# Edge projection beside the first scatter pass, padded lookup tiles and an accumulator kept by products

## The chip, the cores and the metric

The kernel runs on one NeuronCore of one Trainium2 chip. The metric is the device time of one execution in microseconds; lower is better. The core has five engines with an in-order instruction stream each: TensorE (PE; its weight loads are listed as PEld), VectorE (DVE), ScalarE (ACT), GpSimd (POOL) and SyncE (SP, which here only issues DMAs). They meet through semaphores.

## What is computed

A graph network of four layers on one graph of 3125 nodes (256 values each) and 103125 edges, with 18 or 64 attributes, a type and a weight per edge. Each layer normalizes x, gathers rows by edge, and sums messages by node:

```python
N, E = 3125, 103125
edge_index = jnp.stack([src, dst])
h = jnp.maximum(_layernorm(x, axis=-1), 0.0)
x = x + _L0_gnn_ref(h, edge_index, edge_attr_18, ...)       # softmax over the edges of src
h = jnp.maximum(_layernorm(x, axis=-1), 0.0)
x = x + _L1_gnn_ref(h, edge_attr_64, edge_weight, ...)      # softmax over the edges of dst
h = jnp.maximum(_layernorm(x, axis=-1), 0.0)
x = x + _L2_gnn_ref(h, ..., src, dst, edge_type_8)          # typed sum, batch norm
h = jnp.maximum(_layernorm(x, axis=-1), 0.0)
x = x + _L3_gnn_ref(h, src, dst, ...)                       # attention over dst

# inside _L1_gnn_ref, what the change touches:
    ep = ef @ We + be                                       # (E, 64) @ (64, 32)
    scores = jnp.einsum('ehd,ehd->eh', q[dst], k[src] + ep[:, None, :]) * scale
    scores = scores * ew[:, None]
    m = jax.ops.segment_max(scores, dst, num_segments=n)
    ex = jnp.exp(scores - m[dst])
    s = jax.ops.segment_sum(ex, dst, num_segments=n)
    out = jax.ops.segment_sum((ex / s[dst])[:, :, None] * v[src], dst, num_segments=n)
```

## The kernel before

**Sorting.** `sort_all` brings the edges into the order of src and then of dst, by counting. A node number is split into a block (25 of them, `NB`) and a place in it (126, in tiles of P = 128). Edges lie in tiles of 128, and a step is G = 8 tiles; 101 steps (`ISTEPS`) cover all edges. The function runs these blocks one after the other; each ends when all engines have ended their part:

1. Loading (to L321). SyncE loads src, dst, type and weight, each by one main load (L288), five loads of a column each (`RCOL`, L291) and a short last one (L292); then x (L296, L297) and the weights of the edge projection and of the first node projection (L300 to L302). Behind the first two VectorE makes the keys (L316 to L321).
2. Histogram (L374 to L495). Per step VectorE writes two sets of one-hot rows, block (`hi`, 25 wide, L338) and place (`lo`, 128 wide, L340), into a buffer of two rounds of four steps; TensorE counts a round by 32 products of them into one bank (L423, waits for `hist_ready`, signals `hist_used`). Beside it runs the edge projection, edge_attr_64 times We: SyncE loads `feat` (L407), TensorE turns a step by four transposes (`turn`, L434), multiplies by `duo_w` in four products (`multiply`, L443), ScalarE copies the turned tiles (`take`) and the products (`stage`), and stores them to `projected` in DRAM, which layer 1 reads. At the end VectorE and TensorE make the start of each node's segment (`lay_out`, L346 on; `lay_out_sums`, L465).
3. First scatter pass, `scatter(keys_of[0], ..., FirstPass)`: each edge's record is written to its place in the order of src. Step b: SyncE waits until the scatters of step b-2 have landed (L524) and loads the attributes (L526). TensorE turns the block one-hots (L642, copied by ScalarE, L564), spreads the keys (L654, compared by VectorE, L608). Then comes the table chain, four times per step (d = 0 to 3, two tiles each): ScalarE copies the table from PSUM (L577), TensorE updates it with two products (L670) and looks two tiles up in the copy with f32 products over 25 rows (L675), and VectorE picks the base out of each (L616). From rank and base VectorE makes the eight positions (L625), and GpSimd issues eight indirect DMAs, one per tile (L545). `FirstPass` also counts the histogram of the other key: VectorE makes `next_hi` and `next_lo`, TensorE counts them (L717) at d = 3 in bank SPARE. Its hooks `sync`, `tensor_table` and `scalar` are empty. At the start ScalarE issues a DMA that fills the second order's record array with blanks (17120 KB).
4. Second scatter pass, with `SecondPass`, in the order of dst; beside it the layer norm of x and its projection to q, k and v (products of 512 columns) run, spread over the steps.

**Layers.** `edge_layer(kind)` runs layers 0, 1 and 3 (`kind` 0, 1, 3) over 107 steps of eight tiles (T = 856) in sorted order. GpSimd gathers rows of `kv` by indirect DMA (L1120), TensorE expands q by edge (`expand`, L1187 and L1190), VectorE makes key products and weighted messages (L1509, L1476) and scans for maxima (L1444), ScalarE exponentials and one-hots; then TensorE sums messages by node, two tiles per pair into a bank (`sums`, L1230), ScalarE copies the four pair sums to `pair_sums` (`move_sums`, L1357; the last two rows of each go to DRAM, L1360), and VectorE adds each into `acc`, at the pair's block (`add_sums`, L1465). TensorE's order of a step is `expand(2)`, `turn_scores`, `sums(0)` of two steps ago, `expand(3)`, `turn_back`, `expand(0)` of the next step, `sums(1)`, `expand(1)`, `front`. In `expand` the bank goes round; VectorE's key products read it. Layer 2 has its own loop and isn't touched.

## Time and profile before

| | |
|---|---|
| median of 3 runs | 8586.36 us (8586.0 to 8587.62) |
| profiled execution, its own time | 8571.41 us |
| span in its trace | 8569.7 us |
| mean granted TensorE clock | 0.784 |
| TensorE busy | 6613.0 us (77%) |
| VectorE busy | 5308.7 us (62%) |
| ScalarE busy | 3576.5 us (42%) |
| GpSimd busy | 5221.6 us (61%) |

Busy shares are means over stages which have different limits, so they are read by stretch: loading until 55 us, histogram until 285, first scatter pass until 1333, second until 2394, then the layers. The page's line of 40 slices shows the same: the granted TensorE clock stands at 5 tenths through the scatter passes and at 8 to 9 later.

```profile
PE   7999998999979989974777777667855555667675
...
DVE  6677776666657777774999999721122223455556
...
POOL 0477776777767777721777777200277775677772
PEclk9655555555589999997999999879877777887887
```

### The profile page before, as it was taken

Reading aid. Unit: us, or ns where it says so; the run is one execution under the profiler, and the core shown is the slowest. Engines: PE = TensorE matmul, PEld = TensorE weight load, DVE = VectorE, ACT = ScalarE, POOL = GpSimd, SP = SyncE. Lnnn points to the kernel's source line nnn. Section 1 sums busy time; section 2 is a strip of 40 time slices with the busy share of each in tenths; the row PEclk is TensorE's granted clock in tenths of the full one; section 3 lists DMA queues with packets and bytes.
Section 4 is the critical chain, followed back from the end, with each engine's and each line's share of the span. In section 5 each row is a group of like instructions: output and inputs, shape, how many; then the busy total and the mean of one; then the engine's idle time right before and its main releaser. Section 6 shows DMA issues by size and latency. Waiting matters only on the chain. (4 is left out here: it accounts for less than half of the span.)

```text
span 8569.7 us, 143502 instructions
## 1 busy us (share of the span) xinstructions
PE 6613.0 (77%) x33110; PEld 4732.5 (55%) x33111; DVE 5308.7 (62%) x15263; ACT 3576.5 (42%) x10766; POOL 5221.6 (61%) x5120
## 2 busy tenths in 40 slices
PE   7999998999979989974777777667855555667675
PEld 6777775666646666652555555455433344445454
DVE  6677776666657777774999999721122223455556
ACT  3322222333347666632666666223200000777772
POOL 0477776777767777721777777200277775677772
PEclk9655555555589999997999999879877777887887
DMA  7411111111145555532666666200344443444442
GB/s 219 136 17 16 17 17 26 33 33 34 33 106 140 138 136 138 140 61 96 184 175 175 176 178 175 85 11 33 132 108 108 108 108 80 107 110 109 109 108 47
DMA packets 1013468, 849.20 MB, mean 99 GB/s; under 512 B 751678, under 2 KB 841581, under 8 KB 1009339
## 3 DMA queue, kind: packets, MB, share of 16 engines
q0 software_dynamic: 257152, 645.64, 27.7%
q1 hardware_dynamic: 710069, 154.62, 9.1%
q10 hardware_dynamic: 45780, 44.08, 1.5%
q14 instruction: 341, 2.79, 0.1%
q8 instruction: 126, 2.06, 0.1%
HBM read 723.28 MB, written 120.67 MB: 98 GB/s over the span
## 5 line engine op out<-in xcount | busy, mean ns | idle before, releaser
L1120 POOL DMA_INDIRECT edges_kv<-kv,edges_rec x1712 | 1998.4, 1167 | 968.0 <-issue 511.0
L1230 PE MATMUL banks<-edges_kv,edges_hot 128*128 128x288 f32 (+2 forms) x5136 | 1563.8, 455 | 623.3 <-DVE edges_kv L1476 412.9
L1230 PEld LDWEIGHTS banks<-edges_kv,edges_hot 128*128 128x128 f32 x5136 | 1051.9, 215 | 1005.0 <-issue 563.6
L1631 POOL DMA_INDIRECT edges_rows<-rel,edges_rec x856 | 809.3, 945 | 965.2 <-DMA edges_rec<-by_dst_records 710.0
L545 POOL DMA_INDIRECT by_src_records<-sort_by_src_rec,sort_pos_i x808 | 773.9, 958 | 544.2 <-issue 533.2
L1120 POOL DMA_INDIRECT edges_kv<-feat,edges_rec x856 | 829.3, 969 | 270.4 <-issue 253.9
L675 PE MATMUL banks<-sort_table,sort_hot_hi_t 25*128 25x128 f32 x3232 | 952.1, 444 | 52.0 <-DVE sort_junk L616 47.2
L1647 PE MATMUL banks<-edges_rows,edges_hot 128*128 128x256 f32 x1712 | 625.8, 529 | 466.1 <-DMA edges_rows<-rel,edges_rec 449.2
L545 POOL DMA_INDIRECT by_dst_records<-sort_by_dst_rec,sort_pos_i x808 | 773.7, 958 | 288.0 <-issue 250.3
L1465 DVE TENSOR_TENSOR acc<-edges_pair_sums,acc 128x288 f32 (+2 forms) x1284 | 560.6, 437 | 487.0 <-DMA edges_kv<-feat,edges_rec 268.7
L675 PEld LDWEIGHTS banks<-sort_table,sort_hot_hi_t 25*128 25x128 f32 x3232 | 721.5, 307 | 221.2 <-issue 121.1
L1647 PEld LDWEIGHTS banks<-edges_rows,edges_hot 128*128 128x128 f32 x1712 | 428.0, 262 | 664.3 <-issue 404.0
L616 DVE SCALAR_TENSOR_TENSOR sort_junk<-banks,sort_hot_lo 128x128 bf16<-128x128 f32 x1616 | 435.3, 287 | 578.0 <-PE banks L675 537.5
L1330 ACT ACTIVATE edges_off<-columns,edges_column 128x128 bf16<-128x128 f32 x2568 | 784.6, 390 | 0.0
L1679 DVE TENSOR_TENSOR agg<-banks,agg 128x256 f32 x428 | 181.7, 424 | 768.8 <-PE banks L1647 768.8
L1302 ACT ACTIVATE edges_apart<-banks,minus_p 128x512 bf16<-128x512 f32 x642 | 429.3, 686 | 435.0 <-PE banks L1142 226.8
L608 DVE SCALAR_TENSOR_TENSOR sort_junk<-banks,sort_key_cur,sort_earlier 128x128 bf16<-128x128 f32 x1616 | 575.6, 411 | 6.0 <-PE banks L654 6.0
L1357 ACT COPY edges_pair_sums<-banks 128x288 f32<-128x288 f32 (+2 forms) x1284 | 460.7, 383 | 275.6 <-PE banks L1230 246.8
L1476 DVE TENSOR_TENSOR edges_kv<-edges_kv 128x1024 f32<-128x1024 f32 x428 | 518.8, 1212 | 0.0
L577 ACT COPY sort_table<-banks 25x128 f32<-25x128 f32 x808 | 204.8, 254 | 728.2 <-PE banks L670 728.2
L564 ACT COPY sort_hot_hi_t<-banks 25x512 f32<-25x512 f32 x404 | 231.9, 574 | 647.2 <-PE banks L642 647.2
L1190 PE MATMUL banks<-x,edges_hot_t 128*128 x1712 | 476.5, 403 | 3.4 <-DVE edges_kv L1509 3.4
(372 smaller groups left out, 12506.6 us busy)
## 6 DMA issues: line engine op xcount, KB each, us to landing
edges_kv<-kv,edges_rec POOLq DMA_INDIRECT x1712
sort_feat<-in_edge_attr_dram SPq DMA_DIRECT2D x100, 256.0 KB, 3.6
rel<-tables_stage SPq DMA_DIRECT2D x25, 1008.0 KB
by_dst_records<-by_dst_blank ACTq DMA_DIRECT2D x1, 17120.0 KB, 54.2
edges_rec<-by_dst_records SPq DMA_DIRECT2D x107, 160.0 KB
edges_rows<-rel,edges_rec POOLq DMA_INDIRECT x856
edges_kv<-feat,edges_rec POOLq DMA_INDIRECT x856
by_src_records<-sort_by_src_rec,sort_pos_i POOLq DMA_INDIRECT x808, 2.1
```

The source lines that it names most:

```text
L545: pool.indirect_dma_start(O.rec, bass.IndirectOffsetOnAxis(ap=pos_i[:, u, c:c + 1], axis=0), rec[:, u, c, :], None).then_inc(scattered[u], 16)
L608: last = dve.scalar_tensor_tensor(out=junk[:, 0, c, 0:P + mates].rearrange("p (t e) -> p t e", e=P), in0=ps[:, 4 + h, end - P - mates:end] ...
L675: pe.matmul(ps[:, 2 + c % 2, 0:P], hot_hi_t[:, u, c, :], table[:, d % 2, :], start=True, stop=True).then_inc(looked_up, 1)
L1120: pool.indirect_dma_start(kv[:, r, c, 0:koff + DIM], None, tab, bass.IndirectOffsetOnAxis(ap=reci[:, r, c, idx:idx + 1], axis=0)).then_inc ...
L1190: last = pe.matmul(out[:, c, 2 * P - QW:2 * P], hot_t[:, b % 2, 2 * m + c, :], rows, start=(kind == 1), stop=(kind == 1 or c == 1), skip_g ...
L1230: last = pe.matmul(ps[:, 6 + m % 2, 0:OW], hot[:, b % 2, c, :], kv[:, b % BUFS, c, koff:koff + OW], start=(c % 2 == 0), stop=(c % 2 == 1))
L1330: last = act.activation(off[:, c, :], C.columns[:, c % 2, :], ACT.Abs, bias=column[:, b % 2, c:c + 1], scale=-1.0)
L1357: act.copy(pair_sums[:, m, :], ps[:, 6 + m % 2, 0:OW]).then_inc(sums_copied, 1)
L1465: dve.tensor_tensor(rows, pair_sums[:, m, :], rows, ALU.add).then_inc(added, 1)
L1476: dve.tensor_tensor(v4, v4, bc(exps, dh), ALU.mult).then_inc(msg_done, 1)
L1631: pool.indirect_dma_start(rows[:, b, c, :], None, tab, bass.IndirectOffsetOnAxis(ap=reci[:, b, c, idx:idx + 1], axis=0)).then_inc(gathered ...
L1647: last = pe.matmul(ps[:, m, 0:DIM], hot[:, b, c, :], rows[:, b, c, :], start=(c % 2 == 0), stop=(c % 2 == 1))
```

## The change

1. Loading: the five column loads of each array become one (`PARTS = 3`). The loads of x and of the weights move from the loading block to the block of the histogram. GpSimd clears three more tiles.
2. Histogram: the projection leaves it. VectorE writes into `hot_hi` and `hot_lo`, two steps deep, and TensorE counts each step for itself.
3. First scatter pass: `FirstPass` gets the projection. SyncE loads `feat` behind the attribute load of the same step (two buffers). TensorE turns half a step at d = 0 and half at d = 2, and multiplies the half before; ScalarE copies both at d = 1 and d = 3 and issues the store at d = 1. The count of the other histogram moves to the table bank's columns 128 to 255, two tiles at each d, before the table's own products.
4. Both passes: `hot_hi`, `hot_hi_t` and `table` get 128 columns or rows in place of 25, the rest zero; lookups (L675) run over 128 rows, turns (L642) and table products (L670) give 128 rows.
5. Layer 1 (`kind == 1`): a product of the identity with `acc`'s block is added in PSUM to each pair's sum (`with_past`), after a wait for the copy of the pair before (`acc_kept`). ScalarE copies the sum back to `acc` and rows 96 to 127 of it to `pair_sums`. VectorE's additions are gone.

```diff
-        hot_hi = ph.sbuf("hot_hi", [P, 2, G, NB], BF16)
+        hot_hi = ph.sbuf("hot_hi", [P, 2, G, P], BF16)
-        hot_hi_t = ph.sbuf("hot_hi_t", [NB, 2, G, P])
+        hot_hi_t = ph.sbuf("hot_hi_t", [P, 2, G, P])
-        table = ph.sbuf("table", [NB, 2, P])
+        table = ph.sbuf("table", [P, 2, P])
...
-        feat = ph.sbuf("feat", [P, ROUND, G, FA])
-        feat_t = ph.sbuf("feat_t", [P, 2, HALF, P])
+        feat = ph.sbuf("feat", [P, 2, G, FA])
+        feat_t = ph.sbuf("feat_t", [P, 2, P])
...
-        PARTS = RCOL + 2
+        PARTS = 3
...
+                pool.memset(table[:], 0.0).then_inc(filled, 1)
+                pool.memset(hot_hi_t[:], 0.0).then_inc(filled, 1)
+                pool.memset(hot_hi[:], 0.0).then_inc(filled, 1)
...
-                    for g in range(RCOL):
-                        sp.dma_start(tile[:, MAIN + g:MAIN + g + 1], rest[g]).then_inc(loaded[k], 16)
+                        sp.dma_start(tile[:, MAIN:MAIN + RCOL], dram[MAIN * P:MAIN * P + RCOL * P].rearrange("(g p) -> p g", p=P)
+                                     ).then_inc(loaded[k], 16)
...
+                def body(j, b):
+                    dve.wait_ge(hist_used[b], j)
+                    position_ones(dve, keys_of[0], hot_hi[:, b, :, 0:NB], hot_lo[:, b], bass.ds(j * (2 * G) + b * G, G), hist_ready)
...
+                def body(j, b):
+                    pe.wait_ge(hist_ready, j * 4 + 2 * b + 2)
+                    for c in range(G):
+                        last = pe.matmul(ps[0:NB, 0, 0:P], hot_hi[:, b, c, 0:NB], hot_lo[:, b, c, :],
+                                         start=False, stop=False, skip_group_check=True)
+                    last.then_inc(hist_used[b], 1)
...
-                            last = pe.matmul(ps[0:NB, 0, P * c:P * c + P], hot_hi[:, b % 2, 4 * h + c, :], C.ident_b[:],
+                            last = pe.matmul(ps[:, 0, P * c:P * c + P], hot_hi[:, b % 2, 4 * h + c, :], C.ident_b[:],
...
-                                last = pe.matmul(ps[0:NB, TABLE, 0:P], hot_hi[:, u, c, :], hot_lo[:, u, c, :],
+                                last = pe.matmul(ps[:, TABLE, 0:P], hot_hi[:, u, c, :], hot_lo[:, u, c, :],
...
         class FirstPass:
             def sync(sp, j, b, tail):
-                pass
+                u = b % 2
+                if not opening(j, b, 2):
+                    sp.wait_ge(feat_made, at(j, b)(2, 0) - 2)
+                if not tail:
+                    sp.dma_start(feat[:, u], rows_main(feat_dram)[:, bass.ds(at(j, b)(G, 0), G), :]).then_inc(feat_in[u], 16)
...
+            def tensor_table(cls, pe, j, b, d, tail):
+                if opening(j, b, 1):
+                    return
+                if d == 0:
+                    pe.wait_ge(next_ready, at(j, b)(2, 0))
+                last = cls.count(pe, (b + 1) % 2, (2 * d, 2 * d + 1))
+                if d == PAIRS - 1:
+                    last.then_inc(next_used, 1)
...
+            def turn(pe, j, b, h, tail):
+                u = b % 2
+                if h == 0:
+                    pe.wait_ge(feat_in[u], turn_of(j, b) * 16 + 16)
+                for i in range(2):
+                    c = 4 * h + 2 * i
+                    last = pe.transpose(ps[:, SPARE, P * i:P * i + P], feat[:, u, c:c + 2, :].rearrange("p c a -> p (c a)"), C.ident[:])
...
             def tensor(cls, pe, j, b, d, tail):
+                if d == 0:
+                    if not opening(j, b, 1):
+                        pe.wait_ge(feat_taken, n(2, 0))
+                        cls.multiply(pe)
+                    cls.turn(pe, j, b, 0, tail).then_inc(feat_made, 1)
+                if d == 2:
+                    pe.wait_ge(feat_taken, n(2, 1))
+                    cls.multiply(pe)
+                    cls.turn(pe, j, b, 1, tail).then_inc(feat_made, 1)
...
+            def scalar(cls, act, j, b, d, tail):
+                n, u = at(j, b), b % 2
+                if d == 1:
+                    act.wait_ge(feat_made, n(2, 1))
+                    if not opening(j, b, 1):
+                        cls.take_products(act, 1 - u, 1)
+                    cls.take_turned(act).then_inc(feat_taken, 1)
+                    if not opening(j, b, 1):
+                        act.wait_ge(feat_taken, n(2, 1))
+                        act.dma_start(rows_main(projected)[:, bass.ds(n(G, 0) - G, G), :], feat_out[:, 1 - u]).then_inc(feat_stored[1 - u], 16)
+                if d == 3:
+                    act.wait_ge(feat_made, n(2, 2))
+                    act.wait_ge(feat_stored[u], turn_of(j, b) * 16)
+                    cls.take_products(act, u, 0)
+                    cls.take_turned(act).then_inc(feat_taken, 1)
...
+                def with_past(j, b, m):
+                    if not (first_steps(j, b, 1) and m == 0):
+                        pe.wait_ge(acc_kept, n(PAIRS, m))
+                    pe.matmul(ps[:, 6 + m % 2, 0:OW], C.ident[0:BN, :],
+                              acc[0:BN, bass.ds(block, 1), :].rearrange("p o w -> p (o w)"), start=False, stop=True).then_inc(summed, 1)
...
                     if oldest:
                         sums(*oldest, 0)
+                        if kind == 1:
+                            with_past(*oldest, 0)
                     if inside:
                         expand(j, b, (3,))
+                    if oldest and kind == 1:
+                        with_past(*oldest, 1)
...
                     if oldest:
                         sums(*oldest, 1)
+                        if kind == 1:
+                            with_past(*oldest, 2)
                     if ahead:
                         expand(*ahead, (1,))
                     if beyond:
                         front(*beyond)
+                    if oldest and kind == 1:
+                        with_past(*oldest, 3)
...
+                        if kind == 1:
+                            act.copy(acc[:, bass.ds(blocks[m], 1), :].rearrange("p o w -> p (o w)"), ps[:, 6 + m % 2, 0:OW]
+                                     ).then_inc(acc_kept, 1)
+                            act.copy(pair_sums[ENDS:P, m, :], ps[ENDS:P, 6 + m % 2, 0:OW]).then_inc(sums_copied, 1)
+                            continue
```

## Rows read from the trace of the kernel before

**Rows 1.** Stretches, both scatter passes: us; busy PE, PEld, DVE, ACT, POOL; clock; DMA; GB/s.
```profile
285.00:1332.60 1047.60, 973.10 (x5583) 730.00 (x5581) 769.80 (x3699) 272.47 (x1193) 773.88 (x808) 0.50 0.16 28
...
1359.60:2394.30 1034.70, 939.46 (x4918) 647.07 (x4918) 668.78 (x3662) 312.58 (x1465) 773.68 (x808) 0.54 0.16 33
```

**Rows 2.** Timeline, loading stage: start, duration, engine, line, [idle before <-releaser].
```profile
11.26 6.81 SPq L291 DMA_DIRECT2D sort_src_i<-in_src_dram  x5
...
24.56 0.58 DVE L316 TENSOR_SCALAR sort_lo_i<-sort_src_i 128x808 int32<-128x808 int32 x1 [6.89 <-DMA sort_src_i<-in_src_dram]
...
32.99 12.84 SPq L297 DMA_DIRECT2D x<-in_x_dram  x1
...
33.67 0.58 DVE L321 TENSOR_SCALAR sort_by_dst_seg<-sort_dst_i 128x808 f32<-128x808 int32 x1
...
54.92 1.76 SPq L407 DMA_DIRECT2D sort_feat<-in_edge_attr_dram  x4
```

**Rows 3.** Timeline, histogram stage: two pair starts, one count, the end.
```profile
73.22 3.59 PE L423 MATMUL banks<-sort_round_lo,sort_round_hi 128*25 128x128 bf16 x32
...
79.79 0.35 DVE L338 TENSOR_TENSOR sort_round_hi<-banks,sort_by_src_hi 128x200 bf16<-128x200 f32 x1
...
81.19 0.35 DVE L338 TENSOR_TENSOR sort_round_hi<-banks,sort_by_src_hi 128x200 bf16<-128x200 f32 x1
...
263.04 0.28 DVE L346 COPY sort_hist<-banks 25x128 f32<-25x128 f32 x1 [7.77 <-PE banks L465]
```

**Rows 4.** Waits over 55 to 263 us: who waits for whom, us, count, longest.
```profile
DVE sort_round_hi L338 <- PE banks L423: 55.0, 24, 9.4
```

**Rows 5.** Timeline, one step of the first scatter pass.
```profile
1186.62 0.96 POOL L545 DMA_INDIRECT by_src_records<-sort_by_src_rec,sort_pos_i  x1 [0.31 <-issue]
...
1188.48 0.39 PE L670 MATMUL banks<-sort_hot_lo,sort_hot_hi 128*25 128x128 bf16 x2
...
1188.99 10.40 SPq L526 DMA_DIRECT2D sort_by_src_rec<-in_edge_attr_dram  x2
...
1189.01 1.22 PE L675 MATMUL banks<-sort_table,sort_hot_hi_t 25*128 25x128 f32 x4
...
1196.10 0.17 DVE L625 TENSOR_TENSOR sort_pos_i<-sort_base,sort_rank 128x8 int32<-128x8 f32 x1 [0.21 <-DVE sort_junk L616]
```

**Rows 6.** DMA issues: count, KB each, median us from issue to landing.
```profile
sort_feat<-in_edge_attr_dram SPq DMA_DIRECT2D x100, 256.0 KB, 3.6
```

**Rows 7.** Timeline, from positions to first gather in the first pass.
```profile
1009.70 0.17 DVE L625 TENSOR_TENSOR sort_pos_i<-sort_base,sort_rank 128x8 int32<-128x8 f32 x1 [0.21 <-DVE sort_junk L616]
...
1010.67 0.96 POOL L545 DMA_INDIRECT by_src_records<-sort_by_src_rec,sort_pos_i  x1 [0.43 <-issue]
```

**Rows 8.** Timeline: transposes early in the histogram, lookups after a projection product.
```profile
65.72 1.06 PE L434 MATMUL banks<-ident,sort_feat 128*128 128x128 f32 x4
...
1418.45 0.71 PE L675 MATMUL banks<-sort_table,sort_hot_hi_t 25*128 25x128 f32 x4
```

**Rows 9.** Stretches: after a projection product; inside the histogram.
```profile
1418.30:1421.70 3.40, 2.65 (x23) 1.87 (x22) 2.53 (x18) 1.67 (x11) 2.79 (x3) 0.98 0.07 18
...
100.00:262.00 162.00, 161.77 (x1704) 149.63 (x1702) 115.60 (x162) 78.15 (x169) 0.00 (x0) 1.00 0.67 199
```

**Rows 10.** Stretch: the edge stage of layer 1, steady part.
```profile
4200.00:5400.00 1200.00, 911.42 (x4194) 674.85 (x4193) 1117.36 (x1859) 753.40 (x2047) 926.11 (x745) 0.94 0.64 176
```

**Rows 11.** Groups, layer 1, 4200 to 5400 us: busy, mean ns | idle before.
```profile
L1230 PE MATMUL banks<-edges_kv,edges_hot 128*128 128x272 f32 x1488 | 432.0, 438 | 288.6 <-issue 152.0 <-DVE edges_kv L1476 136.2
...
L1465 DVE TENSOR_TENSOR acc<-edges_pair_sums,acc 128x272 f32 x372 | 159.3, 428 | 0.0
...
L1357 ACT COPY edges_pair_sums<-banks 128x272 f32<-128x272 f32 x372 | 132.0, 380 | 57.4 <-PE banks L1230 50.3
```

**Rows 12.** Timeline, layer 1: an addition and what follows it.
```profile
4708.13 0.43 DVE L1465 TENSOR_TENSOR acc<-edges_pair_sums,acc 128x272 f32 x1
...
4708.48 0.41 DVE L1444 TENSOR_TENSOR_SCAN edges_run_max<-edges_pen,banks 64x128 f32<-64x128 f32 x1
```

235 lines of the change are left out of this document (90 added, 145 removed).

## The prediction

> **What bounds the kernel now.** I read the table of stretches first, for the two scatter passes. In the second one GpSimd issues 808 indirect DMAs in 1034.7 us, 1.28 us each, and every other engine has air: that pass is GpSimd's own pace. The first pass has the same 808 and takes 1047.6 us, 10.37 us for each of its 101 steps against 10.24 [rows 1]. TensorE is busy there for 973 of 1047.6 us at a granted clock of 0.50, so two things of nearly equal length run side by side: the gathers' 10.24 and a chain through TensorE, ScalarE and VectorE of 10.3 to 10.4. Then the loading stage, in order of time: VectorE has keys from 24.56 on, but SyncE is held by the load of x (12.84 us) and the next stage begins only at 54.9 [rows 2]. In the histogram the VectorE pairs follow each other at 1.40 us per step; still the stage ends at 263.04, because TensorE also does the edge projection there and VectorE waits 55.0 us in 24 waits for its counts [rows 3, 4]. Last the edge stage of layer 1: in its steady 1200 us there are 93 steps (372 additions at L1465, 4 a step), 12.9 us each; VectorE is busy 1117 us, 93%, TensorE 911 us, ScalarE 753 us, GpSimd 926 us plus its gaps [rows 10, 11]. VectorE is the bound, with GpSimd close.
>
> **The loading stage.** Five column loads per key array become one, and x and the weights go to the next block. SyncE spent 6.81 us on issuing the five columns of src, and VectorE started at 24.56, when the last src load had landed [rows 2]; one column load in place of five should spare about 6 us of that, and VectorE start near 18.5. Its two key conversions took 24.56 to 34.25 with a wait between (the last, L321, starts at 33.67 [rows 2]), so they end near 27.5 and the histogram starts 27 us earlier (22 to 30: the one column load has as many elements as five had, so its own issue may be longer). x is now issued while VectorE builds one-hots; nothing waits for it before the second pass. The three new GpSimd clears lie beside the loads. -27.
>
> **The histogram.** Without projection, VectorE sets the pace: 101 x 1.40 = 141.4 us, plus 3 at the ends, instead of the 208 us from 54.96 to 263.04 [rows 3]. Now that only two steps are buffered, a count of 8 products must end before VectorE has done the next step: 32 took 3.59 us at their slowest [rows 3], so 0.9 and two hand-overs, below 1.40, with little to spare. -63 (-50 if every step loses 0.13). Both together: -90.
>
> **The first pass, where the projection now is.** Per step it adds to TensorE four transposes (the same four took 1.06 us before the clock rose [rows 8]) and four products of about the same length, and to ScalarE two copies of each kind and a store. What counts more is a new wait. SyncE's loop first waits for the scatters of step b-2 to land, issues the attribute load of b, and only then the load of feat for b. TensorE needs that feat right after the first lookups of step b, in the same in-order queue as the table chain. So: scatter b-2, feat load, rest of step b's chain, scatter b. Round the loop: from the first to the last gather of b-2 7 x 1.28 = 9.0 us; from the last gather (1186.62) to SyncE's next issue (1188.99) 2.4; the feat issue behind the attribute load 0.4 (an estimate); landing 3.2 (less than the median of 3.6 in the histogram, where the DMAs had more to do [rows 6]); the rest of the chain R; and 0.8 from the positions (ready at 1009.87) to the first gather at 1010.67 [rows 5, 7]. R before is from 1188.48 to 1196.27, 7.8 us at the lower clock, none of it idle TensorE to speak of; with transposes and products 9.8. At the upper clock a set of lookups takes 0.71 instead of 1.22 us [rows 5, 8], so all of R times 0.58 is 5.7. The loop covers two steps: (15.8 + R) / 2 = 12.8 us per step at the lower clock, 10.75 at the upper, against 10.37 now.
>
> **Which clock.** The tall and wide shapes don't shorten an operation by themselves. The row that matters is the clock: 0.50 in the first pass with TensorE busy 93% on products of 25 rows or 25 columns [rows 1]; 1.00 in the histogram with transposes and products of 128x128 f32 between the narrow counts; and 0.98 in the short stretch after a full 512-column product of the second pass [rows 9]. So busy time alone does not raise it here, full-size work does, and after the change nearly all lookups and turns are full-size. But the new loop leaves TensorE idle for 3 to 4 us in each step, until feat lands, and the work after such a gap starts at the lower level. I take half of R's saving lost after the gap, less what comes back late in it: R = 7.2, hence 11.5 us per step. 101 x (11.5 - 10.37) = +114 us (bounds +38, all at the upper clock, and +245, all at the lower). Start: the blank fill of by_dst saturates the DMAs beside the first steps, so their feat loads land late: +12 (0 to 20). The last stores lie beside the last gathers: 0.
>
> The Trainium skill (TensorE: Matmul & The Clock Gate, "Why this matters for your kernels") asks only for continuous TensorE work to reach the full clock, and warns that an idle gap between bursts brings the lower one back. The first half would have the first pass warm already, and the tall shapes worth nothing; the granted 0.50 there says otherwise, and the measurement decides. The second half is the third rival below, at its 12.8 us.
>
> **The second pass** gets the same shapes and nothing else. It is at GpSimd's pace and stays there: 0 (+-3).
>
> **Layer 1's accumulator by product.** VectorE loses four additions per step; what follows one begins 0.35 us after it [rows 12], so 1.4 of 12.0 busy us, leaving 10.6. TensorE gains four products with the identity, 8 instructions; the same kind at L1230 takes 432.0/1488 = 0.29 us each [rows 11], so 2.3 on top of 911/93 = 9.8: 12.1. ScalarE gains four copies of 0.38 at most [rows 11] on top of 8.1: 9.6. The additions no longer queue behind VectorE's work, but product m now waits for ScalarE's copy of product m-1, and behind that wait stand, on TensorE, the next expansions, which VectorE's key products need. In the present order an expansion (about 1 us) lies between each two, which covers a copy of 0.38 us. So TensorE takes VectorE's place: I take 12.2 us, 107 x (12.2 - 12.9) = -75. Bounds: -150 if all 1.4 us come through; +30 if the copies' wait is exposed (0.3 us a step). GpSimd's gathers there take 926/745 = 1.24 us.
>
> The Trainium skill (SBUF — State Buffer, "SBUF: two separate sides") says a VectorE operation with two SBUF inputs, which these additions are, can lock GpSimd out for its length. The trace agrees so far that a gather takes 1.24 us beside them against 0.96 in the passes; by the rule the gathers would get shorter and the gain nearer the upper bound.
>
> **Sum.** -90 + 114 + 12 - 75 = -39 on the profiled execution's 8571.4 us (span 8569.7 and 1.7 around it): 8532. The median of the runs shown is 15 us above that execution, so 8547; I say **8545 us**.
>
> **Rivals.** (A) The forecast, 0.43. (B) The feat load is hidden: the clock stays up, the loads land in 2.5 us, the loop falls under GpSimd's 10.24, and the first pass ends like the second: -90 - 13 + 12 - 75 = -166, 8420 us. For it: 10.75 is near 10.24, and a faster TensorE makes its own slack. Against: 9.0 + 2.4 + 0.8 of the loop are fixed. 0.20. (C) Slower than before: the gap keeps TensorE at the lower clock through the step, 12.8 us per step: -90 + 245 + 12 - 75 = +92, 8678 us. For it: the 0.50 of both passes now. Against: without a gap left to wait in, there would be more full-size work per microsecond than now. It decides from 10.37 + (90 + 75 - 12)/101 = 11.9 us per step. 0.20. (D) The accumulator gives nothing, since TensorE with its chain of ScalarE copies is as late as VectorE was: 12.9 us again, +36, 8622 us. For it: 12.1 us of TensorE work leaves 0.8 for all its waits, and it had 3.1 idle. Against: its present idle time waits for VectorE, which gets faster. 0.12. What is left, 0.05, is a histogram that runs off its 1.40.
>
> **Chances.** A run of this kernel can tell 0.2% (17 us) from no change. A lies around -39 with some 35 either way: of its 0.43 about 0.32 is faster, 0.09 the same, 0.02 slower. B is faster, C slower, D half same, half slower. Together: faster 0.56, same 0.16, slower 0.28. The range leaves out the outer half of B's and C's errors: 8420 to 8690.
>
> **What would show it.** Histogram: VectorE's pairs at 1.40 us and the first scatter near 195 us. First pass: steps of 11.5 us in the position additions; TensorE idle for 3 to 4 us before the first transposes, ended by the DMA of feat; gathers idle before each eighth; a granted clock of 0.7 to 0.9, in place of 0.50. Second pass: 1035 us, clock well above 0.54. Layer 1: steps of 12.2 us, VectorE under 90% busy and waiting for products of L1190, TensorE over 90%. The prediction falls if SyncE's feat load is not what the first transposes wait for, if the clock sticks at one level, or if layer 1's steps stay at 12.9.

## The result, and the profile after

| | before | after |
|---|---|---|
| median of 4 runs | 8586.18 us (8579.67 to 8587.62) | 8639.69 us (8627.75 to 8646.84) |
| profiled execution | 8571.41 us | 8646.5 us |
| span, mean granted clock | 8569.7 us, 0.784 | 8644.7 us, 0.847 |

The ratio is 1.0063, with a 95% interval of 1.0048 to 1.0079: the change makes the kernel slower by 0.6%, 54 us in the medians and 75 us between the two profiled executions. The forecast was 8545 us, 41 us faster. The stretches below come from the profiled executions, so they hold 21 us more than the medians do.

The two traces are compared by landmarks: the first and last indirect DMA of each pass, and the first instruction of the block behind layer 1.

| stretch | before, us | after, us | difference | forecast |
|---|---|---|---|---|
| start to first scatter | 285.0 | 195.4 | -89.6 | -90 |
| first scatter pass | 1047.6 | 1229.0 | +181.4 | +126 |
| second pass, with what lies before it | 1061.7 | 1056.3 | -5.4 | 0 |
| to the first gather of layer 1 | 1647.4 | 1639.6 | -7.8 | 0 |
| layer 1, first gather to the next block | 1398.7 | 1387.8 | -10.9 | -75 |
| rest, which the change doesn't touch | | | +7.3 | 0 |

The stretches of the kernel after that answer to [rows 1, 10]: busy us of PE, PEld, DVE, ACT and POOL, then granted clock, DMA share, GB/s.

```profile
195.40:1424.40 1229.00, 865.79 (x6789) 705.89 (x6789) 780.46 (x3699) 360.54 (x1596) 776.19 (x808) 0.75 0.25 57
1449.00:2480.80 1031.80, 675.24 (x4918) 562.66 (x4918) 652.12 (x3658) 312.73 (x1464) 775.97 (x808) 0.76 0.16 33
4200.00:5400.00 1200.00, 1074.46 (x5007) 790.93 (x5005) 1039.02 (x1515) 914.72 (x2455) 801.95 (x756) 0.98 0.65 180
```

TensorE has more instructions in the first pass than before (6789 against 5583), and is busy for less time, 866 us against 973: the clock is 0.75 in place of 0.50. Yet the pass is 181 us longer. In the second pass, where only the shapes changed, TensorE's time falls from 939 to 675 us and the pass stays at GpSimd's pace.

The first two stages went as forecast. The timeline of the kernel after: the column load of src, the first key conversion, the start of the next block, two of VectorE's pairs, the end of the histogram.

```profile
11.28 1.26 SPq L289 DMA_DIRECT2D sort_src_i<-in_src_dram  x1
...
20.19 0.58 DVE L306 TENSOR_SCALAR sort_lo_i<-sort_src_i 128x808 int32<-128x808 int32 x1 [1.98 <-DMA sort_src_i<-in_src_dram]
...
28.38 0.37 DVE L371 CAST sort_duo_f<-sort_duo_i 25x428 f32<-25x428 int32 x1 [0.31 <-PEq L263]
...
33.69 0.36 DVE L320 TENSOR_TENSOR sort_hot_hi<-banks,sort_by_src_hi 128x200 bf16<-128x200 f32 x1
35.09 0.36 DVE L320 TENSOR_TENSOR sort_hot_hi<-banks,sort_by_src_hi 128x200 bf16<-128x200 f32 x1
...
175.42 0.28 DVE L328 COPY sort_hist<-banks 25x128 f32<-25x128 f32 x1 [1.23 <-PE banks L404]
```

Against [rows 2, 3]: the column load is issued in 1.26 us in place of 6.81, VectorE starts at 20.2 (forecast 18.5), the block at 28.4 in place of 54.9. The pairs follow each other at 1.40 us and nothing stops them; the histogram ends at 175.4 in place of 263.0.

In the first pass, this is one step that waits and half of the next. The first row is SyncE's attribute load, the second the feat load behind it.

```profile
872.76 0.17 DVE L536 TENSOR_TENSOR sort_pos_i<-sort_base,sort_rank 128x8 int32<-128x8 f32 x1
...
874.61 0.27 PE L642 MATMUL banks<-sort_next_lo,sort_next_hi 128*25 128x128 bf16 x2 [1.83 <-DVE sort_next_lo L322]
...
875.93 0.38 SPq L437 DMA_DIRECT2D sort_by_src_rec<-in_edge_attr_dram  x1
...
876.59 0.34 SPq L615 DMA_DIRECT2D sort_feat<-in_edge_attr_dram  x1
...
879.42 0.69 PE L665 MATMUL banks<-ident,sort_feat 128*128 128x128 f32 x2 [3.11 <-DMA sort_feat<-in_edge_attr_dram]
...
887.58 0.17 DVE L536 TENSOR_TENSOR sort_pos_i<-sort_base,sort_rank 128x8 int32<-128x8 f32 x1 [0.21 <-DVE sort_junk L527]
...
888.59 0.96 POOL L456 DMA_INDIRECT by_src_records<-sort_by_src_rec,sort_pos_i  x1 [3.87 <-DVE sort_pos_i L536]
```

TensorE stands for 3.11 us until feat lands, as forecast for every step; from there to the positions it takes 8.3 us, and GpSimd has been idle for 3.87 us when they come. There is a second wait, 1.83 us, that the prediction didn't name: the count of the other histogram now stands at the head of the step (d = 0), and needs the one-hots that VectorE writes behind its positions of the step before. TensorE's waits from 600 to 1200 us:

```profile
PE banks L642 <- DVE sort_next_lo L322: 95.4, 51, 2.0
PE banks L665 <- DMA sort_feat<-in_edge_attr_dram: 65.8, 25, 5.3
```

The feat wait comes 25 times in these 600 us, so in every second step and not in each, 2.6 us in the mean. A step with it takes 14.8 us, one without it at the upper clock 9.0; they often alternate, and the pair costs 23.8.

The granted clock has two levels here, 1.00 (2.4 GHz) and 0.50 (1.2 GHz). Around the wait of the step shown (columns as above, the clock is the third number from the end):

```profile
872.80:875.50 2.70, 0.89 (x10) 0.81 (x10) 2.67 (x10) 0.41 (x5) 2.09 (x3) 1.00 0.05 9
875.60:879.40 3.80, 0.71 (x4) 0.52 (x3) 2.04 (x8) 0.19 (x2) 2.89 (x4) 0.50 0.49 98
879.42:885.70 6.28, 6.28 (x39) 5.23 (x40) 2.51 (x16) 2.08 (x6) 4.08 (x5) 0.50 0.12 31
```

The clock is already at the lower level when the wait for feat begins (876.3): it fell at 875.5, behind the 1.83 us in which TensorE waited for the one-hots. It stays low over the feat wait and 6.3 us of work behind it.

At the start of the pass there is a hole. The blank fill, and ScalarE's first store of projected rows:

```profile
182.07 0.42 ACTq L180 DMA_DIRECT2D by_dst_records<-by_dst_blank  x1
...
201.19 28.23 ACTq L718 DMA_DIRECT2D edge_projected<-sort_feat_out  x1
...
229.52 0.26 ACT L488 COPY sort_table<-banks 25x128 f32<-25x128 f32 x1 [28.36 <-issue]
...
233.11 0.96 POOL L456 DMA_INDIRECT by_src_records<-sort_by_src_rec,sort_pos_i  x1 [27.71 <-DVE sort_pos_i L536]
```

In layer 1, groups of instructions from 4200 to 5400 us, and below them two score reductions that follow each other in an undisturbed step.

```profile
L1228 PE MATMUL banks<-acc,ident 126*128 x756 | 254.1, 417 | 60.0 <-ACT acc L1364 53.5 <-issue 3.1
...
L1364 ACT COPY acc<-banks 128x272 f32 x378 | 144.1, 381 | 154.6 <-PE banks L1228 137.4 <-DMA ends<-edges_pair_sums 14.9
L1366 ACT COPY edges_pair_sums<-banks 32x272 f32<-32x272 f32 x378 | 143.0, 378 | 9.1
```

```profile
4743.56 2.28 DVE L1547 TENSOR_REDUCE edges_score_raw<-edges_kv 128x64 f32<-128x2048 f32 x1
...
4755.53 2.28 DVE L1547 TENSOR_REDUCE edges_score_raw<-edges_kv 128x64 f32<-128x2048 f32 x1
```

Both kernels have an undisturbed step of about 11.97 us, which is also the median of the 106 steps in both. Only the mean moved, from 12.86 to 12.66. One such step of the kernel before, and two of the kernel after:

```profile
4708.08:4720.05 11.97, 9.20 (x45) 6.86 (x45) 11.97 (x21) 8.16 (x22) 9.25 (x8) 1.00 0.72 191
```

```profile
4743.34:4755.31 11.97, 11.54 (x55) 8.62 (x56) 10.92 (x17) 9.77 (x27) 4.30 (x4) 1.00 0.30 73
4755.31:4767.30 11.99, 11.11 (x53) 7.96 (x51) 10.82 (x17) 9.34 (x26) 9.08 (x7) 1.00 0.61 166
```

Before, VectorE is busy for all of the step. After, no engine is: TensorE comes nearest, with 11.1 to 11.5 us. Per step the products cost 254.1/94.5 = 2.7 us of TensorE (forecast 2.3). And at the end of the layer 10.6 us are lost, from the last scores to the next block 26.4 us in place of 15.8: with nothing left to expand between them, product and copy stand in a row.

```profile
5487.95 0.62 PE L1228 MATMUL banks<-acc,ident 126*128 x2
5488.87 0.39 ACT L1364 COPY acc<-banks 128x272 f32 x1 [1.23 <-PE banks L1228]
...
5489.59 0.72 PE L1228 MATMUL banks<-acc,ident 126*128 x2 [1.01 <-ACT acc L1364]
```

### The profile page after: what moved, and what is told of

It reads as the page before. It is cut to its first block and busy times, and to the rows that moved or that the text cites. A ratio compares the mean times of both kernels' runs of the same rounds, so it can differ in the third digit from the quotient of the medians.

```text
span 8644.7 us, 146268 instructions
## 1 busy us (share of the span) xinstructions
PE 6302.0 (73%) x33965; PEld 4633.2 (54%) x33966; DVE 5189.5 (60%) x14835; ACT 3743.8 (43%) x11397; POOL 5084.2 (59%) x5123
## 5 line engine op out<-in xcount | busy, mean ns | idle before, releaser
L1107 POOL DMA_INDIRECT edges_kv<-kv,edges_rec x1712 | 1850.9, 1081 | 1083.9 <-issue 538.2
L1217 PE MATMUL banks<-edges_kv,edges_hot 128*128 128x288 f32 (+2 forms) x5136 | 1509.2, 443 | 324.7 <-DVE edges_kv L1491 284.3
L587 PE MATMUL banks<-sort_table,sort_hot_hi_t 128*128 128x128 f32 x3232 | 711.9, 356 | 54.1 <-DVE sort_junk L527 54.1
L1480 DVE TENSOR_TENSOR acc<-edges_pair_sums,acc 128x288 f32 (+1 forms) x856 | 378.1, 442 | 480.1 <-DMA edges_kv<-feat,edges_rec 251.4
L587 PEld LDWEIGHTS banks<-sort_table,sort_hot_hi_t 128*128 128x128 f32 x3232 | 576.5, 251 | 73.1 <-DVE sort_junk L527 69.6
L1524 DVE TENSOR_TENSOR edges_kv<-banks,edges_kv 128x256 f32<-128x256 f32 (+1 forms) x856 | 440.0, 552 | 50.9 <-PE banks L1177 20.0
```

Source lines behind the costliest of these rows:

```text
L587: pe.matmul(ps[:, 2 + c % 2, 0:P], hot_hi_t[:, u, c, :], table[:, d % 2, :], start=True, stop=True).then_inc(looked_up, 1)
L1107: pool.indirect_dma_start(kv[:, r, c, 0:koff + DIM], None, tab, bass.IndirectOffsetOnAxis(ap=reci[:, r, c, idx:idx + 1], axis=0)).then_inc ...
L1217: last = pe.matmul(ps[:, 6 + m % 2, 0:OW], hot[:, b % 2, c, :], kv[:, b % BUFS, c, koff:koff + OW], start=(c % 2 == 0), stop=(kind != 1 an ...
L1524: dve.tensor_tensor(k2, by, k2, ALU.mult).then_inc(edges_used, 1)
```

## The experiments

Four open points: what holds the steps of the first pass, what holds its start, whether the padded shapes are worth their place, and what layer 1's products give. Theory 1 is the prediction's loop (scatter of b-2, feat load of b, the chain, scatter of b); its rival is the new wait for VectorE's one-hots.

**Feat load ahead (`early_feat`).** SyncE issues feat of step b before it waits for the scatters of b-2; the load's own condition, `feat_made`, is met long before.

```diff
                         u = b % 2
+                        if beside is FirstPass:
+                            beside.sync(sp, j, b, tail)
                         sp.wait_ge(scattered[u], turn_of(j, b) * P)
...
-                        beside.sync(sp, j, b, tail)
+                        if beside is not FirstPass:
+                            beside.sync(sp, j, b, tail)
```

> The changed kernel, but SyncE issues the feat load of step b before it waits for the scatters of step b-2, not behind the attribute load. Theory 1 (the loop scatter, feat load, chain, scatter sets the first pass): the wait for feat goes, a step costs what those without it cost now, 9.0 us of TensorE's chain at the upper clock, so GpSimd's 10.24 holds; first pass 28 + 101 x 10.24 = 1062 us in place of 1229, time 8473. Rival (the new wait of the count at the head of each step for VectorE's next ones holds it: 1.8 us of idle TensorE in each step, after which the lower clock comes back): steps of 11.2 us, as those steps now that have no feat wait at the lower clock, pass 1160, time 8570.

Measured: 8469.47 us (8467.99 to 8473.42), 0.9877 of before (0.986 to 0.9893). First pass:

```profile
195.30:1253.80 1058.50, 792.86 (x6789) 645.45 (x6789) 774.02 (x3699) 361.18 (x1596) 773.96 (x808) 0.83 0.29 66
```

```profile
PE banks L645 <- DVE sort_next_lo L322: 119.8, 59, 3.5
...
PE banks L668 <- DMA sort_feat<-in_edge_attr_dram: 5.8, 17, 0.5
```

The forecast time of theory 1 was 8473. The pass falls from 1229.0 to 1058.5 us; the wait for the one-hots is still there, and even grows (119.8 us in 600), and costs nothing any more: it is TensorE's slack behind GpSimd. The loop through the feat load is shown, and with it that its place in SyncE's queue, not the work, made the change slower. The clock still falls in the steps, behind the wait for the one-hots (848.8 is the end of one of 1.94 us), but comes back sooner:

```profile
847.00:850.40 3.40, 1.52 (x13) 1.30 (x14) 3.37 (x16) 0.88 (x7) 2.66 (x3) 1.00 0.54 110
850.40:853.80 3.40, 3.40 (x20) 2.42 (x21) 3.02 (x15) 1.09 (x4) 2.48 (x4) 0.50 0.05 10
```

**The count later (`late_count`), and both (`early_late`).**

```diff
-                if opening(j, b, 1):
+                if opening(j, b, 1) or d == 0:
                     return
-                if d == 0:
+                if d == 1:
                     pe.wait_ge(next_ready, at(j, b)(2, 0))
-                last = cls.count(pe, (b + 1) % 2, (2 * d, 2 * d + 1))
+                last = cls.count(pe, (b + 1) % 2, ((0, 1, 2), (3, 4, 5), (6, 7))[d - 1])
```

> The changed kernel, but the count of the other histogram is made at d = 1, 2, 3 (3, 3 and 2 tiles) in place of all four, so TensorE waits for VectorE's next ones one lookup later. Theory 1 (the feat loop alone): TensorE waits for feat as much longer as it waits less for the ones; steps stay at 11.9 us, time 8640 within 10. Rival (the ones' wait): 1.8 us less in each step, 10.3, time 8480. Both together: in between, 8560.

> Both edits: feat load ahead of the wait for the scatters, and the count from d = 1 on. Theory 1 and the rival alike: no wait is left on TensorE's side but GpSimd's pace; first pass 28 + 101 x 10.24 = 1062 us, time 8473, and no faster than the early feat load alone if theory 1 is right. A third (it is TensorE's work itself, at the lower clock, that is too long): steps stay over 11 us.

Measured: `late_count` 8633.49 us, 1.0064 (1.0048 to 1.0081), first pass 1222.9 us; `early_late` 8517.75 us, 0.993 (0.9913 to 0.9947), first pass 1103.2 us. TensorE's waits from 600 to 1200 us, of `late_count` and then of `early_late`:

```profile
PE banks L665 <- DMA sort_feat<-in_edge_attr_dram: 145.8, 51, 4.8
```

```profile
PE banks L590 <- DVE sort_junk L530: 51.7, 56, 0.9
PE banks L557 <- DVE sort_hot_lo L322: 51.0, 56, 0.9
PE banks L645 <- DVE sort_next_lo L322: 35.8, 56, 0.7
```

Alone, the later count turns one wait into the other (145.8 us for feat in place of 65.8) and gains nothing: the rival falls. With the early load it costs 45 us of the pass and the time is 8518 for an expected 8473, which neither theory had: TensorE waits 2.5 us per step in three places in place of 2.0 in one, and its steps go through a pattern of eight with a mean of 10.7 us. A reading that was not tried: the counts at d = 0 fill time in which TensorE would wait for VectorE anyway, and at d = 1 to 3 they stand in the chain.

**Store by SyncE (`early_late_store`, then `best_2`).** SyncE stores the projected rows of step b-2 at its step b, ahead of feat, and ScalarE's store goes. `best_2` has it with the early load, the count where the change put it, and layer 1's additions as before.

```diff
                 if not opening(j, b, 2):
+                    sp.wait_ge(feat_taken, at(j, b)(2, 0) - 1)
+                    sp.dma_start(rows_main(projected)[:, bass.ds(at(j, b)(G, 0) - 2 * G, G), :], feat_out[:, u]).then_inc(feat_stored[u], 16)
                     sp.wait_ge(feat_made, at(j, b)(2, 0) - 2)
...
-                    if not opening(j, b, 1):
-                        act.wait_ge(feat_taken, n(2, 1))
-                        act.dma_start(rows_main(projected)[:, bass.ds(n(G, 0) - G, G), :], feat_out[:, 1 - u]).then_inc(feat_stored[1 - u], 16)
```

> As the one with both edits, and the projected rows are stored by SyncE in place of ScalarE. In the changed kernel ScalarE's first store has an issue of 28.23 us, while the blank fill that the same engine issued moves 17 MB. Theory: the issue is held by the fill on ScalarE's own queue, and on SyncE's it is not: the hole of 28 us between the first and the second eight gathers falls to under 5, time 25 lower than with both edits, 8448. Rival: the DMAs are full, whoever issues: the store or the feat load waits just as long, no gain.

> The kernel of early_store_adds again (early feat load, store by SyncE, additions by VectorE in layer 1), on a chip of the first kind. First pass: theory (the 28 us hole comes from ScalarE's store behind the blank fill on its own queue) 1038 us; rival (the DMAs are full whoever issues) 1058 as with the early load alone. Layer 1 from its first gather to the next block: rival of the forecast (the products gave 11 us, TensorE at 11.97 us a step where VectorE was at 11.97) 1399 us; the forecast's theory (the products gave 75) 1460. Time by theory and rival: 8469 - 20 + 11 = 8460.

Measured: `early_late_store` 8502.56 us, 0.9912 (0.9896 to 0.9929), first pass 1083.5 us, 19.7 less than without it; the time is 15 us less, where 25 was expected, and misses the expected 8448, as `early_late` under it had missed its own. `best_2` 8467.78 us (8456.71 to 8492.06), 0.9865 (0.9849 to 0.9882). Its first pass, SyncE's first store, and its layer 1 from first to last gather:

```profile
195.20:1235.00 1039.80, 792.54 (x6789) 644.33 (x6789) 772.88 (x3699) 355.90 (x1596) 774.19 (x808) 0.84 0.29 68
```

```profile
200.20 0.34 SPq L617 DMA_DIRECT2D edge_projected<-sort_feat_out  x1
```

```profile
3934.80:5317.10 1382.30, 1044.80 (x4746) 772.05 (x4747) 1270.01 (x2100) 857.19 (x2319) 1068.58 (x856) 0.93 0.64 175
```

1038 us was expected for the first pass and 1039.8 came; the store's issue takes 0.34 us where ScalarE's took 28.23, and the hole is gone. The fill moves the same 17 MB in both, at the same time, so the issue was held on ScalarE's own queue, behind the fill that it had issued there, and not by busy DMAs. Layer 1 to the next block takes 1412.2 us (1399 was expected), against 1382.9 with the products (`early_feat`) and 1387.8 (the kernel after); the kernel before has 1398.7 with the same additions. By the traces the products are worth 11 to 29 us there, not 75. The 29 is the weaker number: the profiled execution of `best_2` took 8492.06 us, 24 more than its median. By the ratios `best_2` is some 10 us faster than `early_feat`, of which the store is 19, which leaves the products some 9 us, with intervals of 14 us either way. So `best_2` and `early_feat` are the same within their intervals, and both beat the kernel before and the kernel after. The early load, SyncE's store and the products together were run only on the chips of the last part.

**Narrow shapes (`early_narrow_4`).** As `early_feat`, with lookups, turns and table products over 25 rows or columns again.

```diff
-                            last = pe.matmul(ps[:, 0, P * c:P * c + P], hot_hi[:, b % 2, 4 * h + c, :], C.ident_b[:],
+                            last = pe.matmul(ps[0:NB, 0, P * c:P * c + P], hot_hi[:, b % 2, 4 * h + c, 0:NB], C.ident_b[:],
...
-                                last = pe.matmul(ps[:, TABLE, 0:P], hot_hi[:, u, c, :], hot_lo[:, u, c, :],
+                                last = pe.matmul(ps[0:NB, TABLE, 0:P], hot_hi[:, u, c, 0:NB], hot_lo[:, u, c, :],
...
-                                pe.matmul(ps[:, 2 + c % 2, 0:P], hot_hi_t[:, u, c, :], table[:, d % 2, :],
+                                pe.matmul(ps[:, 2 + c % 2, 0:P], hot_hi_t[0:NB, u, c, :], table[0:NB, d % 2, :],
```

> The kernel of early_narrow again (early feat load, old shapes of 25 rows or columns in both scatter passes). Theory (the full-size shapes raise the clock and that makes room for the projection): granted clock of the first pass 0.5, steps of 11.7 us or more, first pass 1210 us, time 8620. Rival (the projection's own full-size work keeps the clock up, the padding is worth nothing): first pass 1060, time 8470.

Measured: 8816.29 us (8812.74 to 8827.09), 1.0277 (1.026 to 1.0295): 347 us slower than the same kernel with padded shapes.

```profile
198.90:1594.70 1395.80, 1225.94 (x6789) 949.38 (x6789) 811.58 (x3699) 363.58 (x1596) 773.91 (x808) 0.56 0.21 49
1621.80:2655.40 1033.60, 937.74 (x4918) 647.62 (x4918) 668.61 (x3660) 312.80 (x1465) 773.85 (x808) 0.54 0.16 33
```

The instructions are the same in number (6789), the clock 0.56 in place of 0.83, TensorE's time 1226 us in place of 793. So the padding holds the clock up. The projection's own full-size transposes and products hardly do: 0.56 with them, 0.50 in the kernel before without. Which of the three padded shapes counts was not separated. The second pass takes the same time at either clock (1033.6 us, and 1029.9 in `early_feat`). Steps of the first are 13.7 us, longer than the 11.7 expected: TensorE is busy for 12.1 and waits 1.4 for the one-hots. Without the padding, the projection makes this pass 348 us longer than it was before the change, far more than it spares in the histogram.

**Short product (`short_past_3`).** The kernel after, with the identity product over 16 of 272 columns; the sum over earlier pairs is left out for the others.

```diff
-                    pe.matmul(ps[:, 6 + m % 2, 0:OW], C.ident[0:BN, :],
-                              acc[0:BN, bass.ds(block, 1), :].rearrange("p o w -> p (o w)"), start=False, stop=True).then_inc(summed, 1)
+                    pe.matmul(ps[:, 6 + m % 2, 0:16], C.ident[0:BN, :],
+                              acc[0:BN, bass.ds(block, 1), 0:16].rearrange("p o w -> p (o w)"), start=False, stop=True,
+                              skip_group_check=True).then_inc(summed, 1)
```

> The kernel of short_past again (the changed kernel with the product of the identity over 16 of 272 columns; the other columns' sum over earlier pairs is left out). Theory (TensorE's work, 11.5 of 11.97 us, bounds the undisturbed step of layer 1): median step 10.8 to 11.2 us, VectorE's, and 80 to 120 us less, 8540. Rival (the chain product, ScalarE's copy, product counts): median step within 0.2 us of 11.97, time 8620 or more.

Measured: 8614.82 us, 1.0038 (1.0026 to 1.0049). Layer 1 takes 1371.6 us to the next block, 16 less; the median step is 11.93 us.

```profile
4200.00:5400.00 1200.00, 1010.13 (x5074) 769.99 (x5072) 1052.01 (x1528) 926.95 (x2489) 841.86 (x767) 0.96 0.65 182
```

```profile
L1228 PE MATMUL banks<-acc,ident 126*128 x766 | 131.0, 246 | 51.5 <-ACT acc L1365 46.3 <-issue 3.3
```

The products' time halves, by 1.3 us per step (less than the 2 expected: over 16 columns one still takes 246 ns), and the wait for ScalarE's copy stays (46.3 us against 53.5). TensorE's share falls from 90% to 84%. The time misses the theory's 8540 and comes near the rival's 8620, and so does the median step. But the median hides what happened: 50 of the 106 steps are now under 11.8 us, most of them between 11.2 and 11.6, where the kernel after has 16 (two score reductions that follow each other stand below), and the 106 together are 19 us shorter (mean 12.48 us), of which the end of the layer gives 3 back. So TensorE's work does hold the undisturbed step in part, by some 0.5 us; it is not worth the 80 to 120 us of the theory. That the rest hangs on the chain over ScalarE's copy was argued and not tried; the pauses on top of the undisturbed steps stay open too.

```profile
4662.84 2.28 DVE L1548 TENSOR_REDUCE edges_score_raw<-edges_kv 128x64 f32<-128x2048 f32 x1
...
4674.15 2.28 DVE L1548 TENSOR_REDUCE edges_score_raw<-edges_kv 128x64 f32<-128x2048 f32 x1
```

**On other chips.** Eleven of the eighteen runs fell on three chips on which the kernel before itself takes 10324 to 10430 us. VectorE has pauses of up to 14 us there, and ScalarE of up to 18, whose end the trace puts down to no instruction of the core: about one of VectorE's in each step of the two scatter passes, and none before them. GpSimd's issues are as long as ever (0.96 us), and a step of the second pass takes 13.9 to 14.1 us in place of 10.2. What the pauses are stays open. The ratios to the kernel before on the same chip:

| kernel | ratios, with intervals |
|---|---|
| early load, store by SyncE | 1.0009 (0.9989 to 1.0029), 1.0057 (1.0036 to 1.0078), 1.0041 (1.0026 to 1.0056) |
| the same with additions (`early_store_adds`) | 1.0056 (1.0034 to 1.0079) |
| kernel after with additions (`adds_back`) | 1.0026 (1.0003 to 1.0049), 1.0117 (1.008 to 1.0154) |
| early load, narrow shapes | 1.0046 (1.0022 to 1.007), 1.0123 (1.0097 to 1.015), 1.0127 (1.0103 to 1.0152) |
| short product | 1.0017 (0.9994 to 1.004), 1.0099 (1.0073 to 1.0125) |

The edit of `adds_back`, beside taking out `with_past` and its copies in ScalarE's `move_sums`:

```diff
-                    if kind == 1:
-                        gone = None
```

What was expected, in the order of the three chips:

> The changed kernel with the early feat load, the count left where the change puts it, and the projected rows stored by SyncE. Theory (the early load gives 160 us and SyncE's store another 20, as it did behind the two edits together): first pass 1038 us, time 8449. Rival (SyncE's store, which comes ahead of feat in the queue, delays the loads in every step): first pass longer than with the early load alone, time over 8470.

> The changed kernel with layer 1's accumulator as before: VectorE adds the pair sums, no product with the identity. The forecast's theory (the products spare 75 us): time 8639 + 75 = 8714. Rival (from the two traces: layer 1 from its first gather to the next block takes 1387.8 us against 1398.8, so the products give 11 us): 8650, steps at 12.86 us in place of 12.66.

> The early feat load, but lookups, turns and table products of both scatter passes in their old shapes, 25 rows or columns. Theory (full-size shapes raise the clock, and the clock is what makes room for the projection): the granted clock of the first pass falls from 0.84 to 0.5 to 0.6, TensorE's work per step, 9.6 us before the change, grows by the projection's 2, so steps of 11.7 us or more: first pass 1210 us, time 8620; second pass 0.54 again and still 1030. Rival (the projection's own transposes and products keep the clock up, the padding is worth nothing): first pass 1060, time 8470.

> The changed kernel, the product of the identity with the accumulator made over 16 of its 272 columns, all waits and copies as they are; for the other columns the sum over earlier pairs is left out. Theory (TensorE's own work bounds layer 1's steps now, 2.7 us of it in these products): 2 us less work per step, steps at VectorE's 11.0 to 11.5 us plus the stalls, 100 to 130 us less, time 8525. Rival (the chain product, ScalarE's copy, next product is what counts, not the length of a product): steps within 0.2 us of now, time 8620 or more.

> The kernel of early_store again, on a chip where the kernel before takes 8.58 ms (on the last one it took 10.32, and nothing could be told). Theory (the early load gives 160 us and SyncE's store another 20): first pass 1038 us, time 8449. Rival (the store ahead of feat in SyncE's queue delays the loads in every step): time over 8470.

> The kernel of adds_back again. The forecast's theory (the products spare 75 us): the changed kernel's 8640 + 75 = 8715. Rival (from the two traces: they spare 11 us): 8650, steps of layer 1 at 12.86 us in place of 12.66.

> The kernel of early_narrow again. Theory (the full-size shapes raise the clock and that makes room for the projection): granted clock of the first pass falls from 0.84 to 0.5 to 0.6, steps of 11.7 us or more, first pass 1210 us, time 8620. Rival (the projection's own full-size work keeps the clock up): first pass 1060, time 8470. In the slow chip's traces the clock of the second pass can't decide it, since there the waits were others.

> The kernel of short_past again (the product with the identity over 16 of 272 columns; the other columns' sum over earlier pairs is left out). Theory (TensorE's work bounds layer 1's steps): steps of 11.0 to 11.5 us plus the stalls, 100 to 130 us less, 8525. Rival (the chain of product, ScalarE's copy, product is what counts): steps within 0.2 us, 8620 or more.

> The kernel of early_store a third time, on a chip where the kernel before takes 8.58 ms, it is hoped (on two others it took 10.3 to 10.4). Theory (the early load gives 160 us and SyncE's store another 20): first pass 1038 us, time 8449. Rival (the store ahead of feat in SyncE's queue delays the loads in every step): time over 8470.

> The same with layer 1's accumulator as before, by VectorE's additions. The forecast's theory (the products spare 75 us): 75 us slower than early_store_3, 8524. Rival (they spare 11 us, as the two first traces say): 8460, layer 1 from its first gather to the next block at 1399 us in place of 1388.

> The kernel of early_narrow again, on a chip of the first kind. Theory (the full-size shapes raise the clock and that makes room for the projection): granted clock of the first pass falls from 0.84 to 0.5 to 0.6, steps of 11.7 us or more, first pass 1210 us, time 8620. Rival (the projection's own full-size work keeps the clock up, the padding is worth nothing): first pass 1060, time 8470.

No kernel beats the one before there: every ratio is 1 or above, and the early load with SyncE's store, which was expected at 8449 us, is up to 0.6% slower than the kernel before. The theories can't be judged there: against the kernels with the late feat load on the same chip, the early load with SyncE's store gives 13 to 60 us in place of 190. The order stays, with the narrow shapes last, and so do three things of the traces: the granted clock of the second pass is 0.53 to 0.55 with narrow shapes and 0.66 to 0.67 with padded ones; the end of layer 1 takes 15.8 to 17.5 us with additions and 24.7 to 28.1 with products; the first scatter comes at 195 to 199 us. What the edits are worth depends on the chip.

## Why the prediction was wrong, point by point

**Loading and histogram**: right, -89.6 for -90. The two-step buffer holds: 8 products take 1.03 us and VectorE is never stopped by them.

**The first pass**: the loop was right, and shown by the early load; that every step would wait for feat was not, since the loop covers two steps and its wait comes in one of them. Two sizes failed, one here and one at the start of the pass. The steps' mean without the hole is (1229.0 - 28) / 101 = 11.9 us for a forecast of 11.5, which is +40 us. Of the loop, the two issues and the landing are right (0.66 and 2.8 for 0.4 and 3.2), the last gather to the attribute load is 2.3 for 2.4; the term that failed is R, 8.3 us for 7.2. After the feat wait TensorE is at the lower clock for some 6 us of the 8 (until about 885.7 in the step shown: its pair of transposes takes 0.69 us at 879.42 and 0.39 where the clock is up, the four lookup products 1.17 and 0.66). I had lost half of the saving, which is R = 7.75, and had taken another 0.55 off it with no row behind that. The Trainium skill (TensorE: Matmul & The Clock Gate, "Why this matters for your kernels") warns that a gap between bursts brings the lower clock back. The trace agrees in part: the granted clock is 0.75 in this pass and 0.83 once the feat wait is gone, but in the step shown it had fallen before that gap, behind a wait of 1.83 us, and the gap made the low stretch longer. The wait for VectorE's one-hots, which I had overlooked, turned out to cost nothing in idle time (`late_count`, `early_feat`); the clock falls behind it.

**The start of the pass**: +12 was forecast from feat loads that land late; +28 came, and from another cause. I had costed the projection's stores at nothing, beside the last gathers, and not asked what stands in ScalarE's queue at the first of them: the blank fill. A moved DMA has to be costed in the queue that it is moved into, at its first issue too. This term and R's make up the 55 us between +126 and +181.

**The clock**: right in direction and level, 0.75 in the first pass (0.7 to 0.9 forecast) and 0.76 in the second, and shown by the narrow shapes to be the padding's work. That full-size work raises it needs a limit: the projection's alone left it at 0.56. The padding's worth beside the projection, 347 us, I had put no number on.

**Layer 1**: the step that failed is the subtraction. I set TensorE's 12.1 to 12.2 us of work against 12.9, the mean of the steps before, which holds 0.9 us of pauses; VectorE's undisturbed step was 12.0, and I had that number in the same paragraph. 12.1 against 12.0 is no gain, and the pauses come on top as before. The sum of TensorE's work was itself too high, 11.4 us measured (1074.46/94.5), and the undisturbed step came to 11.97 all the same; `short_past_3` puts some 0.5 us of it down to TensorE, and what else holds it stays open. Rival D (nothing is gained, TensorE with its chain of copies is as late as VectorE was) is nearest to what came, -11 us for its 0, at a chance of 0.12. Left out altogether was the end of the layer, 10.6 us, where the cover named for ScalarE's copy, an expansion, is gone. GpSimd's gathers did get shorter, 801.95/756 = 1.06 us in place of 1.24, and with the additions back 1068.58/856 = 1.25. That agrees with the Trainium skill (SBUF — State Buffer, "SBUF: two separate sides"), that two-input VectorE operations hold GpSimd up; but the gain did not come nearer its upper bound, as the prediction had it by that rule: the median step stayed.

**The sum**: -89.6 + 181.4 - 10.9 and -5.9 in the rest is +75, where -90 + 126 - 75 gave -39. The miss of 114 us is 64 from layer 1 and 55 from the first pass, less 6 from the rest. Either alone would have taken the gain away: with layer 1's term as forecast the sum is +11, with the first pass's +20. "Slower" had stood at 0.28, mostly for a first pass at 12.8 us a step (C); it came at 11.9 and with layer 1's gain missing.

## What to carry to other kernels

A load that is moved into a loop belongs ahead of the waits in its queue that it doesn't need: the same work in the same pass cost 181 us behind one wait and 11 us ahead of it. A change of engine is costed against the bound of the undisturbed step, not against the mean with its pauses, and once more at the ends of the loop, where its cover is missing. Zero padding to full tiles can pay where an engine's clock hangs on it. The clock fell from time to time all the same, also where no wait was longer than 0.9 us (`early_late`), and a wait of 3 us for feat kept it down for 10 us in place of 3.

## What the runs showed of the hardware

- Full-size products over zeros: the same number of instructions took TensorE 793 us at a granted clock of 0.83 and 1226 us at 0.56, by the shape of the lookups, turns and table products alone. The projection's four transposes of 128x128 and four products over 128 rows were in each step of both.
- The granted clock fell from 1.00 to 0.50 at 875.5 in the kernel after, behind a wait of 1.83 us and ahead of one of 3.11, and rose at 885.7; with the second wait gone (`early_feat`) a fall of the same kind lasts from 850.4 to 853.8. In `early_late`, where TensorE's longest wait from 600 to 1200 us is 0.9 us, the clock is still 0.50 from 813.1 to 816.4, between two stretches of 6.7 us at 1.00.
- A DMA issue on a queue behind a 17 MB fill of its own engine held that engine for 28.23 us; the same store from SyncE's queue, beside the same fill, was issued in 0.34 us.
- GpSimd's indirect DMAs in layer 1 took 1.24 us each beside VectorE's additions, 1.06 without them, and 1.25 with them back.
- Chips differ: the kernel before takes 8575 to 8586 us on some and 10324 to 10430 us on three others. There the changed kernels have pauses of VectorE of up to 14 us, nearly all in the two scatter passes and none in the histogram.
